# Windowed attention and a gated, mixed feed-forward: turned y kept as one copy from the second batch on, and the first weights mixed inside the gate

## The reference

```python
x = x + _layernorm(_L0_attn_ref(_layernorm(x), w_qkv))     # x1
y = _layernorm(x)                                          # the hidden states
h = jax.nn.relu(einsum('bsh,oh->bso', y, gate_w1) + gate_b1)
g = (einsum('bso,eo->bse', h, gate_w2) + gate_b2).mean(axis=1)   # 8 numbers a batch
mW1 = W1 + einsum('be,efh->bfh', g, TW1)                   # W2, b1, b2 likewise
u = jax.nn.gelu(einsum('bsh,bfh->bsf', y, mW1) + mb1[:, None, :])
out = einsum('bsf,bhf->bsh', u, mW2) + mb2[:, None, :]
x = x + _layernorm(out)
```

## Time and profile before

| | |
|---|---|
| median of 3 runs | 2894.65 us (2893.51 to 2895.97) |
| the profiled execution, its own time | 2897.68 us |
| its span, first to last instruction | 2895.9 us |
| PE busy | 2827.4 us, 98% |
| DVE busy | 2061.3 us, 71% |
| ACT busy | 1711.8 us, 59% |
| POOL busy | 909.8 us, 31% |
| DMA | 722.30 MB, mean 249 GB/s |

### The profile page before, as it was taken

The page is one execution under the profiler, slowest core; times in us unless marked ns, Lnnn a source line. Parts: engine busy times, 40 slices in busy tenths (PEclk is TensorE's granted clock), DMA queues, the critical chain, the costliest instruction groups (busy, mean ns, idle before and its releaser), DMA issues.

```text
span 2895.9 us, 54593 instructions
## 1 busy us (share of the span) xinstructions
PE 2827.4 (98%) x19884; PEld 2361.3 (82%) x19884; DVE 2061.3 (71%) x3808; ACT 1711.8 (59%) x3325; POOL 909.8 (31%) x809
## 2 busy tenths in 40 slices
PE   7999999999999999989989999999999999999998
PEld 6888888888888888777768888788888888878886
DVE  5444444598998999888778666976678676796664
ACT  2222222377777776755546666766668666776666
POOL 2111111289888988954300000500005000130003
PEclk9999999999999999999999999999999999999999
DMA  6776777577877777679998667976579575895642
GB/s 240 239 242 233 240 249 261 189 212 220 231 211 206 205 209 216 192 274 402 394 397 315 228 225 248 365 284 201 200 283 401 204 252 201 299 361 204 217 139 88
DMA packets 340885, 722.30 MB, mean 249 GB/s; under 512 B 27536, under 2 KB 98320, under 8 KB 338720
## 3 DMA queue, kind: packets, MB, share of 16 engines
q1 hardware_dynamic: 304160, 629.40, 64.8%
q0 software_dynamic: 15024, 55.64, 5.5%
q10 hardware_dynamic: 21456, 34.05, 3.4%
HBM read 549.05 MB, written 167.84 MB: 248 GB/s over the span
## 4 chain that ended last, share of the span: by engine, by line
PE 83%; DVE 6%; DMA 4%; issue 3%; ACT 2%; POOL 2%; ACTq 0%; SPq 0%; DVEq 0%; POOLq 0%
PE a_acc L611 17%; PE e_acc L1427 7%; PE e_hid L1410 7%; PE e_acc L1428 7%; PE e_hid L1411 7%; PE e_acc L1429 7%; PE e_hid L1412 7%; PE a_ps_score L660 7%; PE a_ps_keys L677 6%; PE a_ps_out L698 5%; DMA a_gate_att<-o_scratch 2%; PE a_ps_out L706 2%; DVE e_part L1799 1%; PE a_ps_turn L716 1%; DVE a_gate_stats L1678 1%
## 5 line engine op out<-in xcount | busy, mean ns | idle before, releaser
L1799 DVE SCALAR_TENSOR_TENSOR e_part<-e_ring,e_g_cols,e_part 128x512 f32<-128x512 f32 x896 | 652.8, 783 | 4.9 <-DMA e_ring<-mix_rows 2.5
L529 DVE TENSOR_REDUCE a_neg_max<-a_ps_score 128x1 f32<-128x384 f32 (+1 forms) x1024 | 488.9, 529 | 86.2 <-PE a_ps_score L660 82.2
L1823 DVE TENSOR_TENSOR e_u_lo<-e_u,e_u_hi 128x512 fp32r<-128x512 f32 x256 | 179.2, 700 | 373.5 <-ACT e_u_hi L1558 373.4
L1554 ACT ACTIVATE e_u<-e_hid,e_mb 128x512 f32<-128x512 f32 x256 | 176.9, 691 | 431.2 <-PE e_hid L1412 419.6
L448 ACT ACTIVATE a_probs<-a_ps_keys 128x384 f32<-128x384 f32 (+1 forms) x1024 | 417.3, 480 | 20.4 <-PE a_ps_keys L677 9.4
L1283 POOL TENSOR_SCALAR e_var<-e_moments 128x4 f32<-128x4 f32 x15 | 6.8, 450 | 1283.2 <-DVE e_moments L1835 1282.7
L356 POOL TENSOR_TENSOR a_total<-a_probs 128x512 f32<-128x512 f32 x256 | 324.0, 1284 | 97.9 <-ACT a_probs L448 97.8
L660 PE MATMUL a_ps_score<-a_k_st,a_q_st 96*128 96x384 f32 (+1 forms) x1024 | 328.5, 361 | 4.6 <-DVE a_neg_max L529 3.8
L677 PE MATMUL a_ps_keys<-a_q_st,a_k_st 100*128 100x384 f32 (+1 forms) x1024 | 314.7, 350 | 2.7 <-ACT a_probs L448 1.7
L366 POOL TENSOR_TENSOR a_total<-a_total,a_probs 128x512 f32<-128x512 f32 x224 | 287.2, 1284 | 43.5 <-ACT a_probs L448 39.8
L1571 ACT ACTIVATE e_sums<-e_acc 128x512 f32<-128x512 f32 x508 | 289.4, 595 | 8.2 <-PE e_acc L1429 8.2
(11 more groups left out here) (163 smaller groups left out, 6454.2 us busy)
## 6 DMA issues: line engine op xcount, KB each, us to landing
e_ring<-mix_rows SPq DMA_DIRECT2D x558, 512.0 KB, 5.4
qk_scratch<-a_qk SPq DMA_DIRECT2D x128, 512.0 KB, 4.9
a_k_st<-qk_scratch SPq DMA_DIRECT2D x180, 256.0 KB, 4.1
a_q_st<-qk_scratch SPq DMA_DIRECT2D x180, 256.0 KB, 4.1
v_scratch<-a_v SPq DMA_DIRECT2D x64, 256.0 KB, 3.1
a_v_sb<-v_scratch SPq DMA_DIRECT2D x64, 256.0 KB, 4.2
o_scratch<-a_out SPq DMA_DIRECT2D x128, 128.0 KB
x_scratch<-a_gate_x POOLq DMA_DIRECT2D x16, 1024.0 KB, 9.9
```

What stands on the lines that cost most here:

```text
L529: dve.tensor_reduce(neg_max[:, g % 2, i, h:h + 1], ps_score[y % TRIO][:, 0:(hi - lo) * WIN], AX_X, ALU.max, negate=True).then_inc(reduced, 1)
L1799: dve.scalar_tensor_tensor(out=part[:, n % 2, half, :], in0=ring[:, slot, :], scalar=g_cols[:, b, e:e + 1], in1=so_far, op0=ALU.mult, op1= ...
```

## The change

From chunk 4 on (batches 1 to 3) the turned y is stored once, in float32. `yt` has two slots, and a buffer `whole` has two for the plain copy, which ACT takes from PSUM (`stage`) after relu of block 1 and ahead of the square root for y. `high` waits for a store only for chunks 2 to 5, `stage` from chunk 6 on. At the turns `load_y` loads one array, into the place of the low half; ACT copies it to the high half and DVE subtracts in place, in two halves of 1024 elements per partition, four and five steps after the chunk's last `hidden` (`split_y`, `halves_due`). The gate's values of batch 0 are made in rounds 10 and 11; DVE mixes the first half blocks of blocks 0 and 1 in rounds 13 and 14; the order of `hidden`, gate values, mixing and splits after the gate is changed. SP issues the small loads and the first 18 pieces of the ring in round 8 instead of 10, and the loads of y of batch 0 ahead of the first refill. The diff, without lines that only pass `yf_dram` on:

```diff
-    SLOTS = 3
+    SLOTS = 2
+    GATED = CHUNKS - 6
...
-            yt[2] = sb("yt2", [P, 2, KD, CH], F32R, gate_mem)
+            yt[1] = sb("yt1", [P, 2, KD, CH], F32R, gate_mem)
...
-            yt[1] = sb("yt1", [P, 2, KD, CH], F32R, gate_mem)
+            whole = sb("whole", [P, 2, KD, CH], F32, gate_mem)
...
+        staged = sem("staged")
...
         def await_yt(eng, c):
-            eng.wait_ge(yt_stored[c % SLOTS], 32 * (c // SLOTS + 1))
+            eng.wait_ge(yt_stored[c % SLOTS], 32 * (c // SLOTS + 1) if c < PER else 16 * (PER + (c - PER) // SLOTS + 1))
...
-            rows = slice((PER * b + q) * CH, (PER * b + q + 1) * CH)
-            for src, dst in ((yh_dram, y_hi), (yl_dram, y_lo)):
+            await_yt(eng, PER * b + q)
+            if b:
+                rows = slice((PER * (b - 1) + q) * CH, (PER * (b - 1) + q + 1) * CH)
+                pairs = ((yf_dram, y_lo),)
+            else:
+                rows = slice(q * CH, (q + 1) * CH)
+                pairs = ((yh_dram, y_hi), (yl_dram, y_lo))
+            for src, dst in pairs:
...
+        def halves_due(s):
...
+            return [(batch_of(r) + 1, runs[r][1], s - last[r] - 4) for r in range(RUNS)
+                    if closes(r) and batch_of(r) + 1 < BATCH and 0 <= s - last[r] - 4 < 2]
...
+        def half_split(b, q, h):
...
+            return KD * CHUNKS + 2 * (PER * (b - 1) + q) + h + 1
...
             def store_yt(c):
+                if c >= PER:
+                    sp.wait_ge(staged, KD * (c - PER + 1))
+                    sp.dma_start(yf_dram[:, (c - PER) * CH:(c - PER + 1) * CH].rearrange("(k p) t -> p k t", p=P),
+                                 whole[:, c % SLOTS]).then_inc(yt_stored[c % SLOTS], 16)
+                    return
...
-                if k == CHUNKS - 6:
+                if k == GATED - 2:
...
                     for q in range(2):
-                        await_yt(sp, q)
...
-            refill_half(0)
+                if k == CHUNKS - 2:
+                    refill_half(0)
...
-            await_yt(sp, 2)
...
-            await_yt(sp, 3)
...
+                if c > PER:
+                    pe.wait_ge(staged, KD * (c - 1 - PER) + k + 1)
+                if k == 2 and c == GATED + 2:
+                    pe.wait_ge(g_done, 1)
+                elif k == 2 and c == GATED + 3:
+                    pe.wait_ge(cols_done, 1)
...
-                    pe.wait_ge(lo_done, KD * CHUNKS)
+                    pe.wait_ge(lo_done, KD * (GATED + 2))
+                    pe.wait_ge(staged, KD * (GATED + 2 - PER))
...
+                if i == 0:
+                    pe.wait_ge(lo_done, KD * (GATED + 3))
+                    pe.wait_ge(staged, KD * (GATED + 3 - PER))
...
+                else:
+                    pe.wait_ge(lo_done, KD * CHUNKS)
+                    pe.wait_ge(staged, KD * (CHUNKS - PER))
...
                 if jj == 0 and opens(r):
-                    pe.wait_ge(y_loaded[q], 32 * (batch_of(r) + 1))
+                    if batch_of(r):
+                        pe.wait_ge(lo_done, half_split(batch_of(r), q, 1))
+                    else:
+                        pe.wait_ge(y_loaded[q], 32)
...
+                if k == GATED:
+                    gate_values(0)
+                elif k == GATED + 1:
+                    gate_cols(0)
...
-            gate(CHUNKS - 2, 1)
-            gate_values(0)
-            gate(CHUNKS - 2, 2)
-            gate_cols(0)
-            gate(CHUNKS - 2, 3)
+            for m in range(1, KD):
+                gate(CHUNKS - 2, m)
...
+            hidden(1)
...
-            hidden(1)
+            hidden(2)
...
-            hidden(2)
...
         def high(act, c, k):
-            if k == 0 and c >= SLOTS:
+            if k == 0 and SLOTS <= c < PER + SLOTS:
...
+        def stage(act, c):
+            if c >= PER + SLOTS:
+                await_yt(act, c - SLOTS)
+            for k in range(KD):
+                act.wait_ge(lo_done, KD * c + k + 1)
+                act.activation(whole[:, c % SLOTS, k, :], turn[k][:, :], ACT.Copy).then_inc(staged, 1)
...
                 if n == half == 0:
-                    await_yt(act, CHUNKS - 3)
+                    await_yt(act, CHUNKS - 2)
...
-                    for c in range(CHUNKS - SLOTS, CHUNKS):
-                        await_yt(act, c)
...
             for k in range(1, CHUNKS):
+                if k == GATED + 1:
+                    gate_values(0)
...
+                    high_half(1, 0)
...
+                if there(k + 1) and k + 1 >= PER:
+                    stage(act, k + 1)
...
-                    gate_values(0)
                 for m in range(2, KD):
-                    if k == CHUNKS - 1 and m == KD - 1:
-                        high_half(1, 0)
...
-            gate_values(1)
...
+            gate_values(1)
...
+            def split_y(s):
+                for b, q, h in halves_due(s):
+                    if h == 0:
+                        act.wait_ge(y_loaded[q], 16 * (b + 2))
+                    at = slice(2 * h, 2 * h + 2)
+                    act.activation(y_hi[:, y_slot(q), at, :], y_lo[:, y_slot(q), at, :].bitcast(F32), ACT.Copy).then_inc(hi_done, 1)
...
+                split_y(s + AHEAD)
...
             def low_half(n, half):
+                if n == half == 0:
+                    await_yt(dve, CHUNKS - 1)
...
-                if k == CHUNKS - 3:
+                if k == GATED - 1:
...
-            gate_cols(0)
-            mix_half(0, 0, 0, 8)
-            mix_half(1, 0, 0, 2)
+                elif k == GATED + 1:
+                    gate_cols(0)
+                elif k > GATED + 2:
+                    mix_half(k - GATED - 3, 0, 0, EXPERTS)
...
-            mix_half(1, 0, 2, 4)
...
-            mix_half(1, 0, 4, 8)
-            mix_half(0, 1, 0, 6)
...
+            mix_half(0, 1, 0, 4)
...
-            mix_half(0, 1, 6, 8)
+            mix_half(0, 1, 4, EXPERTS)
...
-            mix_half(1, 1, 0, 4)
...
+            low_hidden(1)
...
-            mix_half(1, 1, 4, 6)
-            low_hidden(1)
-            mix_half(1, 1, 6, 8)
+            mix_half(1, 1, 0, 4)
...
+            mix_half(1, 1, 4, EXPERTS)
...
+                for b, q, h in halves_due(s + AHEAD):
+                    dve.wait_ge(hi_done, half_split(b, q, h))
+                    rows = y_lo[:, y_slot(q), 2 * h:2 * h + 2, :]
+                    dve.tensor_tensor(rows, rows.bitcast(F32), y_hi[:, y_slot(q), 2 * h:2 * h + 2, :], ALU.subtract).then_inc(lo_done, 1)
...
-    yh_dram = scratch("yh_scratch", [D, TOKENS])
-    yl_dram = scratch("yl_scratch", [D, TOKENS])
+    yh_dram = scratch("yh_scratch", [D, SEQ])
+    yl_dram = scratch("yl_scratch", [D, SEQ])
+    yf_dram = scratch("yf_scratch", [D, TOKENS - SEQ])
```

4 lines of the change are left out of this document (2 added, 2 removed).

## The result

The kernel after takes 2929.53 us (median of 4 runs, 2924.97 to 2932.20); the kernel before, beside it, 2895.31 us. The ratio is 1.0116 with a 95% interval of 1.0098 to 1.0133: 34 us slower. The prediction said 2912 and at most 2925, so the direction was right and the size was not.

The account below looks back on a forecast made before the run. PE, busy 98%, waits on DVE, so DVE's queue and what it waits for decide. Profiled 2897.68 - 1.8 (front) + 19.7 (turns) = 2915.6, less 3.0 to the median: 2912 us; range 2893 to 2925.

Parts of the forecast that it names:

- Turns: At the three turns between batches, splits make PE wait for u's low half: 7.7, 5.6 and 6.4 us, 19.7 in all.
- the low clock after a wait: At the second turn, six products after a gap take 0.63 us where they take 0.39: 1.4 us.
- ACT's lateness: At the turns, ACT's work coming later adds 0.5 us at the first, 1.3 at the second, 1.6 at the third.
- SP's queue, costed at nothing: Small loads and 18 ring pieces two chunks earlier cost nothing; without an emptied queue chunk 14's rows come up to 7 us late.
- Early chunks and the copies: Gate: ACT's wait at chunk 3 for chunk 1's store costs 6.5 us; second copies in chunks 4 to 13, 4 us.
- The ramp: Start of the feed-forward part: earlier mixing brings the front 12 us if the chunk changes cost nothing.
- The sum wait: Start of the feed-forward part: PE's 7.8 us wait for the gate's sums of batches 1 to 3 goes.
- (a): At the turns, POOL's additions hold each subtraction, so 19.7 us becomes 35: 2928 us, chance 0.12.
- (b): At the turns, subtractions push mixing out of POOL's additions, saving 1.0 us a step; turns cost 7 us: 2893, chance 0.13.
- (d): Turns cheap at 7 us, front as forecast: 2900 us, chance 0.14.
- (c): Turns as forecast, but the early wait vanishes because chunk 1's store lands by 1284: 2904 us, chance 0.11.
- The front's -1.8 us: Up to the feed-forward part's start, all gate losses included: 1.8 us faster, bounds 12 faster and 6 slower.

Follow-up runs that it names:

- the kernel without splits: The kernel after without its 24 ACT copies and 24 DVE subtractions at the turns (y partly wrong): 2897.40 us, ratio 1.0007.
- the copies alone: The kernel after with the 24 ACT copies at the turns kept and the 24 DVE subtractions left out: 2896.41 us, ratio 1.0006.
- The y part alone: The kernel before with only two slots, single stored copy of y and splits at the turns; gate values, mixing, SP's order unchanged: 2924.32 us, ratio 1.0104.
- the execution without splits: The kernel before with the y hunks only, without the copies and subtractions at the turns: 2889.26 us, ratio 0.9976.
- the mixing part alone: The kernel before with only the earlier gate values and mixing, small loads and ring pieces in round 8: 2904.50 us, ratio 1.0037.
- the mixing part with the pieces in round 10: The kernel before with only the gate and mixing hunks, the 18 ring pieces issued in round 10: 2897.74 us, ratio 1.0016.
- the splits within the batch: The kernel before with the y hunks, splits moved to steps 14 to 54 of the batch before, both halves stored: 2895.64 us, ratio 1.0007.

## Why the prediction was right or wrong

**Turns.** The forecast was 19.7 us, measured against the kernel without splits 30.5. Two terms of the sum were too small. The first is the count: of 24 subtractions I charged 15 (six, five, four), each where it stood in a dense stretch ahead of a late low half of u, and took 3.1 us of slack off at the second turn. The price of one, 1.2 us, was right for 17 of them; all 24 together took 36.8 us, and DVE was busier by 25.2, where the sum had 18.0 less 3.1 of slack. The runs show that at a turn there is hardly slack that lasts: DVE is full for the length of it. That mixing which is pushed back is missed by a later step is my reading; no run tries it alone. I had read slack off one step, and it belonged to the whole turn. The second is the low clock after a wait: charged once, 1.4 us at the second turn, it came after waits at all three, and slow products took nearly 10 us more than without splits. The 3.4 us that I added for ACT's lateness were hardly there: the copies alone cost the turns 0.7 us.

**Where PE waits.** I put the wait at the projection, for the low half of u. It came at the hidden layer, for the split y, because a product of the new batch stands in PE's order ahead of that projection. That hid the other wait and did not add to it; moving the splits a step earlier turned the one into the other, for 4 us.

**SP's queue, costed at nothing.** The cover that I named, a queue emptied by 1 MB less a chunk, did not hold: the 18 issues took 11.22 us, as in before. The price that I gave for the loss of that cover, up to 7 us, is the measured wait of 6.96. At PE it became 9.9 us, since ACT and the turned block stand behind DVE. With the pieces back in round 10 it was gone. The gate values in the chunks, also costed at nothing, cost about 1 us.

**Early chunks and the copies.** 5.0 us against 6.5, and 1.0 against 4, of which y's gain was read rightly (1.98 us, forecast 1.9). I had one wait of 8 us at chunk 3 and found three smaller ones; high of chunk 3 started at 1288.26, after the 1284 named.

**The ramp.** The sum wait went and the bias took its place, as forecast: PE waits 4.4 us behind ACT's other gate values, which stand behind the bias. 9.5 us came off against 12. But the mixing was not the only reason. The y part alone brings 7.7 us at the same place (6.0 in the execution without splits), with lighter transfers, and the mixing part alone 6.1; the two do not add up. I had written that this could bring nothing since no wait of PE in the earlier trace rows ends on a DMA. DVE's waits did, and PE's ended on DVE: the step that failed here was to ask only for PE's last releaser.

**The rivals.** (a), POOL holding each subtraction, gave 2928, next to the measured time, but mostly not for its reason: POOL held seven of the 24, for 1.1 us each. (b) fell as a time, but its mechanism was there: the mixing was 11.1 us shorter with the splits, more than POOL's hold cost. (d) fell, all three turns being dear; (c) fell with the early waits, and its sum took 10 us off where the prediction's own terms, 1.8 and 6.5, give 8.3.

By the medians the change adds up so, each term being a difference of two distances from before on the same chip, with some 3 to 6 us of uncertainty: single copy -5.0, earlier gate values and mixing -0.5, ring pieces ahead of the rows +9.7, splits at the turns +30.0: +34.2. By the ratios the four are -6.9, +0.3, +8.7 and +31.6. With the pieces in round 10 the splits cost more, 36.6, so the last two are not independent.

That the sum missed by no more than 17 us is in part luck. The front's -1.8 us was a gain of 12 from the mixing and a loss of 10.5 from slots and copies; the medians have -0.5 and -5.0 for these two. The errors of 11.5 and 15.5 us cancel but for 4.

## What to carry to other kernels

Where an engine is full over a stretch of many steps, charge every instruction added to it in the stretch at its full time; slack read at one step is spent once, not once per step. Where PE is made to wait, add the slow products behind each wait. Take the work to a stretch where that engine waits: the same 24 subtractions cost 36 us at the turns and 7.5 in the middle of a batch, transfers included. A transfer that no one waits for at the end of the chain can still be the wait of the engine that the chain waits for, and the issues behind it in the queue belong to its price. And before a gain is put down to a change, make its last step on the kernel before as well.

## What the runs showed of the hardware

The time that SP needs to issue a DMA is not fixed: a 1 MB load of half of y took 0.36 to 0.85 us to issue in the y part alone and 1.85 to 2.73 us at the same place in before. The DMA engines' busy share there was 0.53 in 1442 to 1445 in the first and 1.05 in 1442 to 1453 in the second. The share does not explain it all: the 18 ring pieces took 11.2 us to issue in after, at a share of 1.06, and 20.8 in the mixing part with the pieces in round 10, at 1.05. An issue of that length holds up whatever the engine does next, on ACT too (3.03 us, and ACT's next copy stood 2.90).

Whether a DVE subtraction of two 128x1024 operands is held by POOL's additions hung on which began first: 2.28 to 2.32 us for the seven that began inside an addition, 1.21 to 1.23 for the 17 that did not.

What stays open: why an earlier front makes the turns dearer by 3 to 6 us. In the traces it goes with DVE, which was busier by 27.1 us there (2076.8 against 2049.7) in place of 25.2, the mixing having given back 6.6 us and not 11.1; why it gave back less was not tried. Open too are the 7.5 us of the splits within the batch, of which ACT's issues are a part that was not separated from what the same step gives to before.
